# Moving the output stores of a tile behind the landing of the next tile's first streamed quarter

## The reference, cut to what matters

```python
x = x + _L0_ffn_ref(_L0_cond_ref(x, L0_cond_weight, ...), L0_ffn_W_base, L0_ffn_b_base, L0_ffn_W_router, L0_ffn_A, L0_ffn_B)
x = x + _L1_ffn_ref(_L1_cond_ref(x, L1_cond_weight, ..., itok_B_1_7), L1_ffn_base_W, L1_ffn_router_W, L1_ffn_lora_A, L1_ffn_lora_B)
return x
```

## Time and profile before

| | us |
|---|---|
| median of 3 runs (912.55 to 915.74) | 915.22 |
| the profiled execution | 914.61 |
| its span | 912.9 |
| PE busy in the span | 902.9 (99%) |
| DVE busy | 615.9 (67%) |
| ACT busy | 313.0 (34%) |
| POOL busy | 145.8 (16%) |
| queue q1, the DMAs of SP: 159.19 MB | 51.0% of 16 engines |
| mean rate of all DMAs | 210 GB/s |

### The profile page before, as it was taken

One profiled execution on the slowest core, in us unless ns is written; L12 is line 12 of the kernel. 1 busy time (PEld: TensorE's weight loads), 2 busy tenths in 40 slices (PEclk: granted clock), 3 DMA queues, 4 the chain that ended last, 5 costly groups with the idle time before them and its releaser, 6 DMA issues.

```text
span 912.9 us, 13364 instructions
## 1 busy us (share of the span) xinstructions
PE 902.9 (99%) x4672; PEld 786.6 (86%) x4672; DVE 615.9 (67%) x1311; ACT 313.0 (34%) x502; POOL 145.8 (16%) x298
## 2 busy tenths in 40 slices
PE   8999999999999999999999999999999999999998
PEld 7999998888998888888888888888788888888886
DVE  6889899766577859976465565565565565556563
ACT  5678778411324424231321221221222222222220
POOL 0100010111002001414213213113113113213110
PEclk9999999999999999999999999999999999999999
DMA  8523330765512033656797787897888888887874
GB/s 337 210 76 120 119 125 23 271 197 172 135 50 93 6 133 96 213 210 230 273 288 256 273 287 247 281 286 255 275 274 265 278 264 270 283 274 261 282 229 177
DMA packets 63090, 191.51 MB, mean 210 GB/s; under 512 B 10664, under 2 KB 13100, under 8 KB 61104
## 3 DMA queue, kind: packets, MB, share of 16 engines
q1 hardware_dynamic: 52448, 159.19, 51.0%
q0 software_dynamic: 10432, 31.35, 11.7%
q10 hardware_dynamic: 144, 0.13, 0.1%
HBM read 158.93 MB, written 32.23 MB: 209 GB/s over the span
## 4 chain that ended last, share of the span: by engine, by line
PE 91%; DMA 7%; DVE 1%; SPq 1%; ACT 0%; issue 0%; DVEq 0%
PE bank L852 24%; PE bank L518 15%; PE bank L520 15%; PE bank L519 15%; DMA t_lo<-t_scratch 6%; PE bank L826 5%; PE bank L835 4%; PE bank L663 2%; PE bank L909 2%; PE bank L923 2%; PE bank L922 2%; PE bank L924 2%; PE bank L580 1%; DMA m_raw<-m1t 1%; PE bank L769 1%; PE bank L565 0%
## 5 line engine op out<-in xcount | busy, mean ns | idle before, releaser
L852 PE MATMUL bank<-g_hi,xs 128*128 128x512 f32 x448 | 145.1, 395 | 0.0
L852 PE MATMUL bank<-t_hi,xs 128*128 128x512 f32 x336 | 114.1, 397 | 1.8 <-DMA t_lo<-t_scratch 1.6
L489 POOL DMA_DIRECT2D p1sel<-p_scratch x128 | 65.6, 512 | 279.0 <-issue 279.0
L852 PEld LDWEIGHTS bank<-g_hi,xs 128*128 128x128 f32 x448 | 83.2, 188 | 16.5
L954 ACT ACTIVATE xs<-x_raw 128x1024 fp32r<-128x1024 f32 x60 | 62.0, 1056 | 81.1 <-PE bank L852 55.7
L852 PE MATMUL bank<-g_lo,xs 128*128 128x512 f32 x224 | 88.3, 394 | 0.0
L1277 DVE TENSOR_TENSOR xs<-x_raw,xs 128x1024 fp32r<-128x1024 f32 x60 | 75.0, 1270 | 17.0 <-ACT xs L954 16.5
L518 PE MATMUL bank<-gx,xs 128*128 128x304 f32 x256 | 77.4, 302 | 0.0
L520 PE MATMUL bank<-gx,xs 128*128 128x304 f32 x256 | 77.4, 302 | 0.0
L519 PE MATMUL bank<-gx,xs 128*128 128x304 f32 x256 | 77.3, 302 | 0.0
L852 PEld LDWEIGHTS bank<-t_hi,xs 128*128 128x128 f32 x336 | 62.0, 188 | 17.6 <-DMA t_lo<-t_scratch 5.5
(11 more groups left out here) (321 smaller groups left out, 2061.2 us busy)
## 6 DMA issues: line engine op xcount, KB each, us to landing
t_hi<-t_scratch SPq DMA_DIRECT2D x82, 512.0 KB, 4.7
t_lo<-t_scratch SPq DMA_DIRECT2D x82, 512.0 KB, 5.8
x_raw<-xq SPq DMA_DIRECT2D x16, 1024.0 KB, 6.9
out<-ost SPq DMA_DIRECT2D x64, 256.0 KB, 5.3
p1sel<-p_scratch POOLq DMA_DIRECT2D x64, 192.0 KB, 4.6
w_raw<-wall SPq DMA_DIRECT2D x16, 512.0 KB, 4.7
w<-e_scratch SPq DMA_DIRECT2D x6, 1024.0 KB, 5.2
ea<-e_scratch POOLq DMA_DIRECT2D x8, 644.0 KB, 4.3
```

The source lines that it names most:

```text
L489: pool.dma_start(f(p1sel[b][STK * s:STK * s + STK, cs]), p1_dram[bass.ds(i * STK, STK), cs]).then_inc(sems[b], 16)
L852: mm = nc.tensor.matmul(bk[j][:], l[:, c, :], m[:, c, :], start=first and c + k == 0, stop=c + k == KH + 1, skip_group_check=True)
```

## The change

The four stores of a tile are taken out of their two places (banks 3 and 0 at the end of the tile, banks 2 and 1 behind T4 in the next) and issued together in the next tile, behind T4 and ahead of T3. Ahead of them SP waits until both halves of T4 have landed. The stores of the last tile stay at its end.

```diff
             load_x(3)
-            store_out(1, (3, 0))
             for tau in range(REG, NT2):
                 n = tau - REG
                 load_t(4, 6 * n + 1)
-                store_out(tau - 1, (2, 1))
+                for h in range(2):
+                    sp.wait_ge(ld_t[h], 32 * (3 * n + 1))
+                store_out(tau - 1, (3, 0, 2, 1))
                 load_t(3, 6 * n + 3)
                 if tau + 1 < NT2:
                     load_t(1, 6 * n + 5)
                 if tau + 2 < NT2:
                     load_x(tau + 2)
-                store_out(tau, (3, 0) if tau + 1 < NT2 else (3, 0, 2, 1))
+            store_out(NT2 - 1, (3, 0, 2, 1))
```

## The result

| | before | with the change |
|---|---|---|
| median of 5 runs | 913.64 us (912.55 to 915.74) | 925.92 us (920.32 to 926.39) |
| ratio | | 1.0125, 95% interval 1.0106 to 1.0145 |
| the profiled execution (span) | 914.61 us (912.9) | 920.32 us (918.6) |

The change makes the kernel 1.25% slower. The forecast was 922.6 us in a range of 911.3 to 931.0, with 0.62 on slower by over 0.5%. The profiled execution is the fastest of the five; the other four took 925.7 to 926.4.

What follows compares the result with a forecast made beforehand. PE was taken as the bound, DMA waits costing only 3.8 us. Losing those and adding 11.2 us of T3 lateness gave +7.4 on 914.6, so 922.0; with 0.6 for the median, 922.6 us, range 911.3 to 931.

Steps and rivals of the forecast that it cites:

- The ceiling of 3.8 us: PE's ten waits for the streamed buffer cost 3.8 us, 0.4% of the time, all DMA can give back in the tiles.
- T4 lands 0.9 us earlier: With no stores ahead, T4's loads issue 0.3 us earlier and stream 0.6 us faster; five or all six waits go.
- The queue serves SP's transfers one behind the other: Assumption on SP's queue: T3's bytes wait behind the four stores and begin about 0.8 us later.
- T3's first load 0.6 us late: SP issues four stores in 2.5 us after T4's landing, so T3's first load goes out 0.6 us late.
- T3 lands 1.0 us later: T3's landing slips 0.8 us behind the stores' bytes plus 0.2 for a slow start; bounds 0 and 2 us.
- the 0.2 us for a slow start: At T3's stream start, the slow start behind stores that T4 had: 0 to 0.6 us, taken as 0.2.
- 0.8 us a tile: T3's lateness of 1.0 us less its 0.25 us margin costs PE 0.75 to 0.8 us; 11.2 us over 14 tiles.
- The sum: Whole kernel: -3.8 us for all waits of today plus 11.2 for T3's lateness gives +7.4 us.
- fit the hole: Rival: T4 lands by 615.8, stores fill the DMA hole before T3; 911.4 us, or 911 to 913; chance 0.16.
- the point of decision: T4's landing 9.0 us after the tile's start decides whether the stores fit the hole before T3.
- The third rival: T3's lateness feeds on itself through POOL's narrow p1sel loads beside its tail: +18.6 us, 933.8; chance 0.14.
- What was to be seen: First store within 0.2 us of T4's landing, T3's first load 0.5 to 1 us later, T3 late in nearly all tiles.

Runs made afterwards that it cites:

- e10_small_no_wait: The change without its wait for T4, and with each store writing only 32 of its 512 columns; 909.92 us, ratio 0.9953.
- e2_wait_21_only: The kernel before, with the wait for T4's landing put ahead of the stores of banks 2 and 1 alone; 915.78 us, ratio 1.0032.
- e1_no_wait: The change without its wait: four stores between T4 and T3, issued at once behind T4's loads; 914.15 us, ratio 0.9996.
- e3_behind_t3: The change without its wait and with all four stores moved behind T3, ahead of T1; 919.11 us, ratio 1.0056.
- e6_p1_late: The change, with POOL's four narrow p1sel loads moved from beside T3's tail to behind the wide ones, at the tile's end; 925.21 us.
- e5_change_again: The change itself, unaltered, run once more for a second profile; 929.53 us in the median of four.

## Why the prediction was right, step by step

- **The ceiling of 3.8 us.** Right. e10_small_no_wait took the waits down to 0.6 us and gained 4.3 us (0.47%, interval 0.31% to 0.62%).
- **T4 lands 0.9 us earlier.** The size was right: 11.02 to 10.06, and all six waits went. That the size came out was partly luck, for the cause was half wrong. I put all of it on the two stores ahead of T4. By e2_wait_21_only against the change these cost some 10.63 - 10.06 = 0.6 us, and the two behind some 11.02 - 10.63 = 0.4. "The queue serves SP's transfers one behind the other" is the sentence that failed: e1_no_wait and e3_behind_t3 show that a load is slower with stores queued behind it.
- **T3's first load 0.6 us late.** It came out right by luck, 12.08 - 11.48 = 0.60 on average. The forecast took one tile for all. In that tile T4 was to land at 616.3, 9.5 us after its start, and landed at 617.07 - 607.28 = 9.8; the average is 10.06. Four stores were to cost SP 2.5 us, and cost 1.80 in that tile and 12.08 - 10.06 = 2.0 on average. The two errors cancel in the average.
- **T3 lands 1.0 us later.** 1.1 us in the first profile, 1.5 in the second, 1.4 in that of e6_p1_late. This term was too small, and it is the mis-sized term of the sum. The stores were to be down 4.1 us after the first issue, since those at the end of the kernel had landed 2.0 to 2.1 us after theirs, and T3's bytes to begin 0.8 us later. With T3's loads behind them, the last store landed 5.0 us after the first issue on average. By the packets' records, the first twentieth of T3's packets had started at 13.15 us into the tile before, at 14.45 with the change and at 14.56 in e5_change_again: 1.3 to 1.4 us later. From there to the start of the last twentieth T3's stream took 5.4 us before, and 5.3 and 5.5 us in these two profiles. So T3's bytes start later than forecast, but the stream as a whole isn't slower; the 0.2 us for a slow start was not the part that fell short.
- **0.8 us a tile.** 34.81 - 34.04 = 0.77 in the first profile; 1.17 in the second and 35.11 - 34.04 = 1.07 in that of e6_p1_late.
- **The sum.** Against its own execution, -3.8 + 11.2 = +7.4 was forecast and 920.3 - 914.6 = +5.7 measured: 14 x 0.77 = 10.8, less 3.8, less 1.2 because tile 2 started at 434.4 us and not at 435.6. Against the medians it is +12.3, so the forecast step of +7.4 was 4.9 us short. The forecast of 922.6 looks better, 3.3 us short of 925.9, only because it started from a median of before that came out 1.6 us high (915.22, then 913.64). With the second profile's lateness the same sum gives 14 x 1.17 = 16.4, less 3.8, +12.6. With that of e6_p1_late, whose total can be used, it is 14 x 1.07 = 15.0, less 3.8, +11.2 on 914.6, and 925.7 was measured. So the mechanism forecast accounts for the medians, with T3's lateness at 1.4 to 1.5 us.
- **The rivals.** The stores did not fit the hole: T4's earliest landing in the first profile was 9.64 us, and 9.0 was the point of decision. By the Trainium skill, DMA: Bandwidth & Descriptors, section Anatomy of one DMA, T4 would have landed 6.8 us after its first issue, as an estimate; it took 10.06 - 1.56 = 8.5 us with nothing else issued on SP's queue meanwhile. The measurement decides. The page gives these figures for DMAs that GpSimd issues, and T4 is SP's, so the prediction had stretched them. Nor do the 2.0 to 2.1 us in the earlier trace rows agree as closely as it said: they are the whole of a store of 256 KB, bytes included, for which the page's sum gives 2.6, again as an estimate. The third rival's time was not far off, but its mechanism fell with e6_p1_late.
- **What was to be seen.** The first store 0.04 us behind T4's landing, T3's first load 0.6 us late, no wait at T4, T3's second half late in 12 and then in 14 of 14 tiles, 11.9 us of waits: all as written. Not foreseen were the waits at T3's first half, 0.8 us in two tiles of the first profile and 4.2 in seven of the second.

## What to carry to other kernels

Before a transfer is moved behind a wait for another transfer's landing, look at what stands behind it in the same queue, and how much margin that has; here the DMA engines ran at 66 GB/s around T4's landing, and that hole was paid by the next load. If a load needs protection from what is queued behind it, wait for a part of it: here the wait for the first half kept SP's issues clear of the next load and gave 0.2%, where the wait for all of it cost 1.25%. And add up the engine's real waits, not the chain's share of DMA: 7% of the chain were 0.4% of the time.

## What the runs showed of the hardware

- A load is slower with stores queued behind it on the same queue. Four stores of 256 KB, issued while a load of four DMAs was under way with nothing ahead of it, made its second half land 1.0 us later (T4, 10.06 to 11.08) and 1.1 us later (T3, 20.14 to 21.23). In the tile shown the load ran at 201 GB/s in place of 322 before any packet of the stores was recorded. With stores of 1/16 the size T4 landed at 10.31, which is hardly outside the spread of 10.06 to 10.24 with none behind it.
- Where 1 MB of writes was issued right ahead of T3, the engines moved 262 GB/s at a DMA share of 1.06 in the 2 us in which T3's stream started, and 336 at a share of 0.92 with nothing ahead. The last of four such stores landed 4.8 us after its issue there, and 2.0 to 2.1 us at the end of the kernel, where nothing followed.
- The lateness of T3 with the change differed by 0.4 us a tile between two profiled executions. Nothing measured here says why.
